# Row maxima of an attention kernel from two-part products, two heads at a time in row tiles of 64

## The reference

```python
# inputs float32; x: (8, 1024, 256)
xn = _layernorm(x)
x = x + attention0(xn) + experts0(xn)      # experts0: relu(xn W1[e] + b1[e]) W2[e] + b2[e], top 2 scores as weights
xn = _layernorm(x)
x = x + attention1(xn) + experts1(xn)      # experts1: xn We[e] + be[e], top 2 of the softmax gates, rescaled
# attention: 16 heads of 16; causal; softmax over keys, with the row maximum subtracted
scores = scale * einsum('bhtd,bhsd->bhts', Q, K)
probs  = exp(scores - max over keys of scores)
out    = (probs @ V / sum over keys of probs) @ Wo
```

## Time and profile before

| | us |
|---|---|
| median of 3 runs | 3083.53 |
| the runs | 3082.11 to 3085.61 |
| span of the profiled execution | 3081.5 |
| PE busy | 2982.1 (97%) |
| DVE busy | 2421.1 (79%) |
| ACT busy | 1972.9 (64%) |
| POOL busy | 1191.8 (39%) |
| PE, all maxima (L1160), sum of the records | 972.2 |

### The profile page before, as it was taken

The page is one execution under the profiler, slowest core; times in us unless marked ns, Lnnn a source line. Parts: engine busy times, 40 slices in busy tenths (PEclk is TensorE's granted clock), DMA queues, the critical chain, the costliest instruction groups (busy, mean ns, idle before and its releaser), DMA issues.

```text
span 3081.5 us, 62739 instructions
## 1 busy us (share of the span) xinstructions
PE 2982.1 (97%) x19312; PEld 1582.3 (51%) x19312; DVE 2421.1 (79%) x7517; ACT 1972.9 (64%) x4954; POOL 1191.8 (39%) x1424
## 2 busy tenths in 40 slices
PE   6999999999999999999999999999999999999998
PEld 3555545444565554545455555454545556544443
DVE  7777788887777878888777887878888777787884
ACT  2666666666666666666666666666666666666665
POOL 3325234252523525335252342534435243252533
PEclk8999999999999999999999999999999999999999
DMA  5766455363655645446374554635547465453642
GB/s 166 208 180 198 133 152 156 109 191 115 187 170 145 178 136 162 132 123 186 110 211 140 166 165 134 176 110 152 178 117 212 138 176 161 126 164 109 170 137 66
DMA packets 276876, 473.27 MB, mean 154 GB/s; under 512 B 52960, under 2 KB 185792, under 8 KB 274496
## 3 DMA queue, kind: packets, MB, share of 16 engines
q1 hardware_dynamic: 236928, 379.48, 40.9%
q0 software_dynamic: 29952, 81.83, 10.2%
q10 hardware_dynamic: 9664, 7.93, 0.9%
HBM read 344.19 MB, written 130.03 MB: 154 GB/s over the span
## 4 chain that ended last, share of the span: by engine, by line
PE 81%; DVE 10%; issue 4%; ACT 3%; POOL 1%; DMA 0%; ACTq 0%; DVEq 0%; POOLq 0%
PE po L1210 17%; PE pmx L1160 15%; PE pst L1147 13%; PE pst L1194 10%; PE pmx L1290 6%; PE pst L1179 5%; DVE pmx L879 4%; PE pst L1301 4%; PE pmx L1249 3%; PE pst L1168 3%; PE pmx L1228 2%; PE pst L1216 2%; DVE rmax L875 1%; ACT probs L722 1%; ACT oraw L751 1%
## 5 line engine op out<-in xcount | busy, mean ns | idle before, releaser
L722 ACT ACTIVATE probs<-pst 128x512 f32<-128x512 f32 (+3 forms) x3072 | 1401.8, 497 | 413.5 <-PE pst L1147 409.7
L621 POOL TENSOR_SCALAR_AFFINE_SELECT probs<-probs 128x512 f32<-128x512 f32 x512 | 326.7, 638 | 1464.7 <-ACT probs L722 1463.6
L875 DVE TENSOR_REDUCE rmax<-pmx 128x1 f32<-128x512 f32 x1024 | 671.1, 683 | 127.6 <-PE pmx L1160 121.0
L1147 PE MATMUL pst<-qs,k_first 98*128 98x512 bf16 (+3 forms) x2048 | 688.6, 342 | 8.7 <-ACT probs L722 4.3
L1160 PE MATMUL pmx<-k_first,qs 96*128 96x512 bf16 (+2 forms) x2048 | 668.0, 343 | 16.1 <-DVE rmax L879 5.0
L879 DVE CUSTOM_DVE_ANT_0 pmx<-pmx,mask,rmax 128x128 f32<-128x128 f32 (+3 forms) x1024 | 534.5, 555 | 162.7 <-PE pmx L1160 152.9
L1210 PE MATMUL po<-probs,v 128*32 128x512 f32 (+3 forms) x6144 | 657.5, 500 | 4.2 <-POOL probs L621 4.1
L879 DVE CUSTOM_DVE_ANT_0 pmx<-pmx,mask 128x128 f32<-128x128 f32 (+3 forms) x1024 | 483.4, 510 | 125.7 <-PE pmx L1160 124.5
L594 POOL DMA_INDIRECT xg<-xn_rows,rows_of x368 | 357.9, 973 | 95.7 <-issue 51.4
L1160 PEld LDWEIGHTS pmx<-k_first,qs 96*128 96x128 bf16 x2048 | 198.6, 98 | 348.0 <-issue 122.5
L1160 PE MATMUL pmx<-k_second,qs 96*128 96x128 bf16 (+3 forms) x1024 | 304.2, 301 | 17.5 <-DVE otok L1016 8.7
(11 more groups left out here) (143 smaller groups left out, 3626.4 us busy)
## 6 DMA issues: line engine op xcount, KB each, us to landing
wt<-w_tiles SPq DMA_DIRECT2D x161, 513.0 KB
qk_parts<-parts SPq DMA_DIRECT2D x256, 192.0 KB
y_slots<-ys SPq DMA_DIRECT2D x368, 128.0 KB
wt<-w_tiles SPq DMA_DIRECT2D x184, 256.0 KB
qs<-qk_parts SPq DMA_DIRECT2D x128, 192.0 KB
xn_rows<-xn SPq DMA_DIRECT2D x16, 1024.0 KB, 6.4
qs<-qk_parts SPq DMA_DIRECT2D x128, 128.0 KB
k_first<-qk_parts SPq DMA_DIRECT2D x64, 192.0 KB, 3.8
```

The lines of the kernel that those rows point to most:

```text
L621: pool.affine_select(out=tri, in_=tri, compare_op=ALU.is_ge, fill=0.0, base=0, pattern=[[0, GH], [1, P]], channel_multiplier=-1).then_inc( ...
L722: act.activation(probs[:, u % 2, j, 0:w], ps[:, 0:w], ACT.Exp, scale=DH ** -0.5).then_inc(st_read, 1)
L875: dve.tensor_reduce(rmax0[:, col:col + 1], src, AX_X, ALU.max).then_inc(mx_read, 1)
L1147: pe.matmul(ps[:, 0:w], keys[0:SROWS, j, k % HT * P:(k % HT + 1) * P], qs[0:SROWS, set_no(q, n) % QRING, j, a:a + w], start=True, stop=Tru ...
```

## The change

The maxima are made from the two leading parts of queries and keys only: four products of parts, 64 rows, where six products and 96 rows were used. The scores keep all six. The stack of heads 0 and 1 starts at partition 0 with these four products (rows 0 to 63), the other two at 64 to 95, the maxima at 96. The stack of heads 2 and 3 is mirrored: the four products lie in partitions 64 to 127, the other two at 32 to 63, the maxima at 0 and 1, and zeros between; its scores are products of 128 rows. A product of maxima has a row tile of 64 by 128, at row 0 for heads 0 and 1 and at row 64 for heads 2 and 3. `pieces_of` lists the pieces so that a piece of the upper side and an equally wide one of the lower side come one after the other, into different banks.

On PE all four pieces of a step are written first; `turn_tokens` moves behind the scores of head 0; `attend` moves to the end of the step, behind `turn_output` and the gate products. On ACT `exponentials` of head 0 stands ahead of `take_tokens`. On DVE `split_projection` and `add_attention` stand behind the fourth maximum. A stack is loaded by four transfers (keys) or six (queries), rows of 2048 bytes. The first use has a few more memsets.

```diff
-    return [(j, t, a, min(a + BANK, (t + 1) * P)) for a in range(0, (c + 1) * BANK, BANK)
-            for j in range(GH) for t in range(c * HT, (c + 1) * HT)]
+    return [(side[i], c * HT + t, a, min(a + BANK, (c * HT + t + 1) * P)) for a in range(0, (c + 1) * BANK, BANK)
+            for i in range(len(SIDES[0])) for two in ((0, 3), (1, 2)) for t in two for side in SIDES]
...
+                for side, heads in enumerate(SIDES):
+                    dst = buf[:, heads[0]:heads[-1] + 1].rearrange("p h t -> p (h t)")
+                    main = dst[MAIN_AT[side]:MAIN_AT[side] + MAIN]
...
             def step(g):
+                if unit(g):
+                    exponentials(*unit(g), 0)
                 if tile_turned(g):
                     take_tokens(*tile_turned(g))
-                if unit(g):
-                    exponentials(*unit(g), 0)
...
-                pe.matmul(bk[:, 0:b - a], qs[0:STACK, set_no(q, n) % QRING, j, t % HT * P:(t % HT + 1) * P],
-                          keys[0:STACK, j, 0:b - a], start=True, stop=True).then_inc(mx_full, 1)
+                main = slice(MAIN_AT[j // len(SIDES[0])], MAIN_AT[j // len(SIDES[0])] + MAIN)
+                pe.matmul(bk[:, 0:b - a], qs[main, set_no(q, n) % QRING, j, t % HT * P:(t % HT + 1) * P],
+                          keys[main, j, 0:b - a], start=True, stop=True).then_inc(mx_full, 1)
...
             def step(g):
-                work = maxima_at(g)
-                if tile_turned(g):
-                    turn_tokens(*tile_turned(g))
+                for piece in maxima_at(g):
+                    maxima(*piece)
                 for j in range(GH):
-                    for piece in work[j:j + 1]:
-                        maxima(*piece)
...
                     if unit(g):
                         scores(*unit(g), j)
+                    if j == 0 and tile_turned(g):
+                        turn_tokens(*tile_turned(g))
...
-                if unit(g - 1):
-                    attend(*unit(g - 1))
                 for c, q in at_step(g, OT):
                     turn_output(q, c)
...
+                if unit(g - 1):
+                    attend(*unit(g - 1))
```

More of the change, by code:

```diff
@@ L185, in uses @@
     for g in range(BEGIN, NR * NU + END - NU):
-        if tile_turned(g):
-            st["tokens", *tile_turned(g)] = len(st)
-        work = maxima_at(g)
+        for q, n, k in maxima_at(g):
+            mx["max", q, n, k] = len(mx)
         turns = at_step(g, TURN)
         for j in range(GH):
-            for q, n, k in work[j:j + 1]:
-                mx["max", q, n, k] = len(mx)
             if j == 2:
@@ L205, in uses @@
                 st["unit", *unit(g), j] = len(st)
+            if j == 0 and tile_turned(g):
+                st["tokens", *tile_turned(g)] = len(st)
             if j == 0 and tile_hidden(g):
@@ L384, in attention_moe_kernel @@
         k_ones = sem("k_ones")
+        side_rows = sem("side_rows")
         dve_done = sem("dve_done")
@@ L459, in load_stack @@
                 sp.wait_ge(qk_stored[g // 2], (q * CH + c + 1) * 64)
[L460 to L466, removed]
+                src = qk_dram[q % 2, c, g, m].rearrange("a (d s h) t -> s a d (h t)", s=len(SIDES), h=len(SIDES[0]))
+                for side, heads in enumerate(SIDES):
+                    dst = buf[:, heads[0]:heads[-1] + 1].rearrange("p h t -> p (h t)")
+                    main = dst[MAIN_AT[side]:MAIN_AT[side] + MAIN]
+                    if m == 0:
+                        sp.dma_start(main, src[side, 0:2].rearrange("a d f -> (a d) f").unsqueeze(0).broadcast_to(
+                            [2, 2 * DH, len(heads) * BANK])).then_inc(s, 16)
+                    else:
+                        for a in range(2):
+                            sp.dma_start(main[a * 2 * DH:(a + 1) * 2 * DH], src[side, 1 + a].unsqueeze(0).broadcast_to(
+                                [2, DH, len(heads) * BANK])).then_inc(s, 16)
+                    rest_rows = dst[REST_AT[side]:REST_AT[side] + REST]
+                    sp.dma_start(rest_rows, src[side, 0:3:2]).then_inc(s, 16)
             def scores_done(q, u):
@@ L489, in load_maxima @@
                 sp.wait_ge(mx_read, mx_done("turn", q, n))
-                for a in range(MROWS):
-                    row = qs[STACK + a:STACK + a + 1, set_no(q, n) % QRING].rearrange("p h (n q) -> p (h n) q", q=P)
-                    sp.dma_start(row, mT[a * GH * HT:(a + 1) * GH * HT, :]).then_inc(mrow_loaded, 16)
+                if (q, n) == (0, 0):
+                    sp.wait_ge(side_rows, 1)
+                for side, heads in enumerate(SIDES):
+                    dst = qs[MAX_AT[side]:MAX_AT[side] + MROWS, set_no(q, n) % QRING, heads[0]:heads[-1] + 1]
+                    rows = MROWS * len(heads) * HT
+                    sp.dma_start(dst.rearrange("p h (n q) -> p (h n) q", q=P),
+                                 mT[side * rows:(side + 1) * rows]).then_inc(mrow_loaded, 16)
             def store_xn(q):
@@ L1086, in step @@
                                 gates(q, part)
-                    if m == 2:
-                        for (c, n), q in at_step(g, PROJ):
-                            split_projection(q, c, n)
-                        for b, q in at_step(g, Y):
-                            add_attention(q, b)
+                for (c, n), q in at_step(g, PROJ):
+                    split_projection(q, c, n)
+                for b, q in at_step(g, Y):
+                    add_attention(q, b)
                 for q, n in set_ended(g):
```

40 lines of the change are left out of this document (24 added, 16 removed).

## The result

| | before | after |
|---|---|---|
| median of 4 runs, us | 3082.82 | 3644.1 |
| the runs, us | 3079.24 to 3085.61 | 3641.6 to 3646.96 |
| span of the profiled execution, us | 3081.5 | 3645.1 |
| ratio of the times, 95% interval | | 1.1817 (1.1803 to 1.1832) |

The account below looks back on a forecast made before the run. The prediction took PE's pace to bound the kernel; -250 + 92 + 218 + 10 = +70 us on 3081.5, the median 2 us above the span, gave 3154 us, 2.3% slower, with its own range of 3090 to 3235.

Parts of the forecast that it names:

- Point 5: Stack transfers, shorter DRAM rows, moved products, clock and memsets: all judged to cost nothing.
- Point 1: Products of maxima on PE: two row tiles work at the same time and halve 500 us, -250 us.
- the tiles don't overlap: Rival on PE's row tiles: no time saved on the maxima, about 3400 us; chance 0.07.
- the second rival: DVE sets the pace, PE standing still for banks at the step's head: 77 us on top, about 3230; chance 0.09.
- Point 2: Changes of tile shape on PE, three a step instead of two: 0.12 us in 768 steps, +92 us (0 to 184).
- Points 3 and 4: Scores waiting for ACT to free their banks, +218 us, and DVE emptying the four banks of maxima, +10 us.
- The new waits don't cost it: PE's clock: stays granted at 1.00 despite the new waits, so no cost.
- point 3: Scores in PE's step lose the maxima between them and wait for ACT to free banks: +218 us (115 to 328).
- The faster rival: PE's waits for DVE vanish and those for ACT stay at the lower bound: -100 us, about 2984; chance 0.22.
- the signs that were to show the prediction wrong: PE waiting for ACT in fewer than half of the steps, a block taking 0.86 us, or DVE's busy share rising.

Follow-up runs that it names:

- e4: The kernel before with only the new order of instructions on PE, ACT and DVE, its six-part maxima and loads kept: 3353.82 us, ratio 1.0873.
- e5: e1 with the maxima on rows 0 to 95 of the whole array, so no third shape and no overlap: 3362.67 us, ratio 1.0902.
- e6: e1 with all four pieces of maxima in the row tile at row 0, so third shape but no overlap: 3413.75 us, ratio 1.1072.
- e1: The changed kernel with its stack loads' slowest source dimension 16 or 32 instead of 2, same bytes and row length: 3290.78 us, ratio 1.0675.
- e9: e1 with DVE reading only half of the columns of each piece of maxima: 3186.12 us, ratio 1.0335.
- e10: e6 with DVE reading only half of the columns of each piece of maxima: 3369.32 us, ratio 1.0927.
- e3: The kernel before with two thirds of its stack bytes loaded from sources with a slowest dimension of 2: 3220.78 us, ratio 1.0442.
- e7: e1 with one pair of maxima ahead of score 0 and one ahead of score 2, two more shape changes a step: 3180.91 us, ratio 1.0332.

## Why the prediction was wrong

The runs give a path from before to after in medians: 3083 to 3363 for the new order, with at most 9 us for the longer loads (e4, e5); +51 for the third shape (e6); -123 for the overlap (e1), 3291; +353 for the pattern of the loads, 3644.

**Point 5, "Edits at nothing", is the step that failed.** It counted SP's transfers and the bytes in the mean DMA share, and asked whether there was room: "Half as long rows in DRAM: the DMA share is 0.21 to 0.57, enough room." The mean over 16 engines can't answer this, since a transfer that only few of them carry takes long beside idle ones. The step never asked how long one stack takes to land: it was 4.8 us before and is 15.6 after, with the stacks issued 3 to 5 steps of 4 us ahead. The 4.8 are covered well, the 15.6 are not for 42 of the 64 stacks of `k_first`. It named what would happen without cover ("weights and expert tiles would be late"), and that is seen too, 26.4 us at L1200, but as the smaller part; the first maxima of a set wait 183.7 and 62.6 us. SP still waits 579 us for ACT at the line of the earlier trace rows (now L538), so the cover that was named was there and was not what mattered: most of the time went behind the issue, in the transfer (from the start of a stack's last issue to its landing 12.7 us, in e1 2.6). The shape of each access pattern in the diff (a broadcast of two copies outermost) had to be read, and was not. Without this step the forecast of 3154 stands against 3291, still outside the range.

**Point 1, -250: right in the block, wrong in the sum.** The block halves exactly, and "the tiles don't overlap" is refuted. The kernel gained 123 us. 60 of the missing 127 were taken back by DVE, as e9 and e10 show; the place is the one that the second rival names, the banks at the step's head, and its size is near the rival's 77. The Trainium skill, TensorEngine Tiling (Array Packing), PSUM Bottleneck, says that tiling speeds up TensorE but not the emptying of PSUM; the 60 us agree with that. Of the other 67, some 40 are further waits for banks inside the blocks, and the rest stays unexplained.

**Point 2, +92: right in the block, 41 us high in the sum.** One more shape change is 0.11 us in the blocks, 768 of them 84 us; 51 of it reached the time (e6 against e5), inside the stated 0 to 184. No price was paid among the four pieces of a block.

**Points 3 and 4, +228: right in cause, low in size.** e4 measured 269. The bank takes 1.14 us and the steps wait as they were walked through.

**The clock.** "The new waits don't cost it" held for the short waits: in e4 all slices but the first are at 9 tenths. It failed for the long ones, which are a part of 353: PE's busy time is 98 us longer than in e1 for the same instructions, at a mean clock of 0.941 against 0.987. By the trace's record of the clock, 48 of PE's 54 longest idle times were followed by a stretch at the lower level.

So of the terms, -250 should have been -123 and +228 rather +270; with +51 for the shape they give 198 without the loads, near the 208 by which e1 is above before. The direction was right because of point 3, not because of what cost most. The faster rival needed point 3 below 150 us; it was 269 with DVE's part. None of the signs that were to show the prediction wrong came: PE waits for ACT in 426 of the 768 steps, the block of four 512-column pieces takes 0.43 us and 0.11 for the change of shape, and DVE's share fell from 79% to 66%. They watched the four priced points and left out the fifth.

**Where the idle time stood.** PE waits 306 us for loads in the changed kernel (issue 192, DMA 114) and 14 in e1. Of the 306, 183.7 are stacks of `k_first` that are late themselves and 62.6 stacks of queries; of the remaining 60, 40 wait for weights of the expert tiles and 11 for the negated maxima, which SP issues from the same queue.

**Left open.** How the lateness in e3 divides between fewer transfers and slack; some 27 of the 67 us missing from the overlap; and in e7 how the 76 us of waits at the maxima and the 57 of idle time overlap, and so what is left of the 61 us.

## What to carry to other kernels

When an edit changes how a buffer is loaded, read the outermost dimension of both access patterns of each transfer; the mean DMA share and the byte count say nothing about a transfer that few engines carry. Products that stand in a row share their banks in a row: before moving what lies between them, time one use of a bank from the product's start to its return, and multiply by the steps. What two row tiles save on TensorE arrives only as far as the reader of their banks keeps up, here half of it.

## What the runs showed of the hardware

- A slowest dimension of 2 in the source pattern of 64 and 128 KB transfers cost 353 us in a program of 3291, and also held up the queue that issues them: one issue took up to 4.45 us in the rows above, and 5.1 at the longest, where e1 has 1.9. A stack landed 15.6 us after its first issue instead of 4.7.
- While PE, DVE and ACT stood still for 6 us, the DMA share was 0.37.
- Two row tiles of 64 rows work at the same time without a visible loss: 0.38 us instead of 0.65 for a block, of which 0.11 is the change of shape in both.
- After a stall of 3.6 us TensorE's clock was granted at 0.58 over 6 us; over the whole execution the mean was 0.941 instead of 0.987, and PE's busy time 98 us longer for the same instructions.
